# Row maxima and row sums of an attention stage sent through small DMA transfers, and three of four score steps started from a bank that ScalarE has filled

## The reference

```python
def _L0_conv_ref(x, gn_gamma, gn_beta, w_qkv, w_proj, b_proj):
    B, C, H, W = x.shape                      # 2, 256, 64, 64
    nh = NUM_HEADS                            # 4
    d = C // nh                               # 64
    xn = group_norm(x, gn_gamma, gn_beta)
    qkv = jnp.einsum('bchw,oc->bohw', xn, w_qkv).reshape(B, 3, nh, d, H * W)
    q, k, v = (qkv[:, 0], qkv[:, 1], qkv[:, 2])
    scores = jnp.einsum('bhci,bhcj->bhij', q, k) * d ** (-0.5)
    attn = jax.nn.softmax(scores, axis=-1)
    out = jnp.einsum('bhij,bhcj->bhci', attn, v).reshape(B, C, H, W)
    proj = jnp.einsum('bchw,oc->bohw', out, w_proj) + b_proj[None, :, None, None]
    return xn + proj
```

## Time and profile before

| | before |
|---|---|
| median of three runs | 5492.59 us (5486.8 to 5498.76) |
| the profiled execution | 5486.11 us |
| its span in the trace | 5484.3 us |
| TensorE busy | 4957.6 us, 90% |
| VectorE busy | 3959.3 us, 72% |
| GpSimd busy | 2966.1 us, 54% |
| ScalarE busy | 2793.4 us, 51% |
| attention loop, first batch element | 139 to 1333 us of the span |
| attention loop, second batch element | 1498 to 2690 us |

### The profile page before, as it was taken

One profiled execution on the slowest core, in us unless ns is written; L12 is line 12 of the kernel. 1 busy time (PEld: TensorE's weight loads), 2 busy tenths in 40 slices (PEclk: granted clock), 3 DMA queues, 4 the chain that ended last, 5 costly groups with the idle time before them and its releaser, 6 DMA issues. The chain is left out here.

```text
span 5484.3 us, 73719 instructions
## 1 busy us (share of the span) xinstructions
PE 4957.6 (90%) x22320; PEld 2313.6 (42%) x22320; DVE 3959.3 (72%) x6354; ACT 2793.4 (51%) x4750; POOL 2966.1 (54%) x2339
## 2 busy tenths in 40 slices
PE   7999999999899999999978869969978996999788
PEld 3333333333333333333346657745544553554344
DVE  4788888883588888888333334458887886898898
ACT  2666666664266666666411111135544554555455
POOL 0555555555055555555437757746645664665675
PEclk9999999999999999999978879989999998999899
DMA  2000000000000000000134435569969998998998
GB/s 73 1 1 1 1 1 1 1 1 34 30 1 1 1 1 1 1 1 1 37 87 128 128 111 163 162 242 365 388 268 350 371 389 304 378 387 350 396 410 358
DMA packets 320271, 812.24 MB, mean 148 GB/s; under 512 B 70094, under 2 KB 137556, under 8 KB 319758
## 3 DMA queue, kind: packets, MB, share of 16 engines
q0 software_dynamic: 193536, 679.59, 32.8%
q1 hardware_dynamic: 126478, 129.39, 6.9%
HBM read 708.40 MB, written 100.43 MB: 147 GB/s over the span
## 5 line engine op out<-in xcount | busy, mean ns | idle before, releaser
L653 POOL TENSOR_TENSOR arena<-arena 128x1024 f32<-128x1024 f32 x480 | 1168.0, 2433 | 955.2 <-ACT arena L1310 952.6
L1841 DVE TENSOR_REDUCE arena<-ps 128x2 f32<-128x1024 f32 x1024 | 1252.2, 1223 | 457.5 <-PE ps L805 454.2
L705 POOL DMA_INDIRECT arena<-corners,arena x1152 | 1094.2, 950 | 687.6 <-issue 301.6
L1310 ACT ACTIVATE arena<-ps 128x1024 f32<-128x1024 f32 x1024 | 995.4, 1022 | 611.2 <-PE ps L834 609.4
L2065 DVE SCALAR_TENSOR_TENSOR ps<-arena,ps 128x256 f32<-128x256 f32 x2304 | 956.3, 483 | 230.9 <-DVEq L2059 220.9
L1172 PE MATMUL ps<-arena 128*128 128x512 f32 x2304 | 1047.5, 598 | 0.2
L834 PE MATMUL ps<-arena 64*128 64x512 f32 x4096 | 977.9, 590 | 19.0 <-ACT ps L1293 19.0
L847 PE MATMUL ps<-arena 128*64 128x512 f32 x4096 | 991.3, 605 | 0.0
L1503 ACT ACTIVATE ps<-arena 128x256 f32<-128x256 f32 x1152 | 500.2, 469 | 471.0 <-DMA arena<-corners,arena 208.4
L689 POOL DMA_INDIRECT arena<-corners,arena x576 | 544.8, 946 | 275.5 <-issue 244.3
L1860 DVE TENSOR_TENSOR arena<-arena 128x1024 f32<-128x1024 f32 x480 | 630.5, 1314 | 79.3 <-ACT arena L1310 79.3
(11 more groups left out here) (165 smaller groups left out, 4108.5 us busy)
## 6 DMA issues: line engine op xcount, KB each, us to landing
corners<-arena SPq DMA_DIRECT2D x256, 256.0 KB
arena<-corners,arena POOLq DMA_INDIRECT x1728, 7.7
img<-in_x SPq DMA_DIRECT2D x8, 1024.0 KB, 9.3
corners<-arena SPq DMA_DIRECT2D x128, 64.0 KB, 2.2
arena<-in_wd SPq DMA_DIRECT2D x2, 2304.0 KB, 8.5
between<-img SPq DMA_DIRECT2D x4, 1024.0 KB, 5.9
arena<-between SPq DMA_DIRECT2D x4, 1024.0 KB, 10.5
resid<-img SPq DMA_DIRECT2D x8, 512.0 KB, 3.4
```

Source lines behind the costliest of these rows:

```text
L653: pool.tensor_tensor(SUMS[u % 2][:, 0], SUMS[u % 2][:, 0], PAIR[g % 2][:, :, 0], ALU.add).then_inc(sum_a, 2)
L705: pool.indirect_dma_start(G3[4 * k + t].rearrange("p a c -> p (a c)"), None, table256[b], bass.IndirectOffsetOnAxis(ap=IS3[:, k, t:t + 1], ...
L1310: af(P[n % 4].rearrange("p h q -> p (h q)"), ps[:, 2 * (n % 2):2 * (n % 2) + 2, :].rearrange("p h q -> p (h q)"), ACT.Exp, scale=float(D) ...
L1841: v.tensor_reduce(mxp[i % 2][:, :, j], ps[:, 4:6, :], AX.X, ALU.max).then_inc(mx_done, 1)
```

## The change

The maxima no longer pass through TensorE and ScalarE. VectorE joins eight maxima (`MNEG`) and a new small multiply of 128 by 2 elements scales them into f16 (`MROWS`). SyncE sends them, four times for each block, to a row in DRAM (`send_row`), and once for each block reads that row back into all 128 partitions (`spread_rows`) of one of two tables `MWIDE`, laid out as query by head. Both the `COEF` matmuls and the seeds now read `MWIDE`, the first with a step of two elements.

The row sums of all blocks but the last also go through DRAM: `RC` is written out, read back as 128 by 8 elements (`SINV`), inverted by one reciprocal, written out and read back into 128 partitions. GpSimd joins the two partial tables (`fold`), so that `row_sums` is half as long.

ScalarE now seeds three of four steps, and each seed stands right behind the exponential that frees its two banks.

```diff
+        row_buf = nc.dram_tensor("row_buf", (2, 2 * CHUNK), F16, kind="Internal").ap()
+        sum_buf = nc.dram_tensor("sum_buf", (2, CHUNK), F32, kind="Internal").ap()
+        inv_buf = nc.dram_tensor("inv_buf", (2, CHUNK), F32, kind="Internal").ap()
...
-        MWIDE = att.f32(2, CHUNK, dt=F16)
-        MSTAT = att.f32(128)
+        MWIDE = [att.f32(CHUNK, 2, dt=F16) for _ in range(2)]
+        MNEG = att.f32(2)
+        MROWS = [att.f32(4, 2, dt=F16) for _ in range(2)]
+        SINV = att.f32(2, 4)
...
-        def seeds_in(g):
-            return 2 * g + 3 if 2 * g + 3 < STEPS else None
+        def is_seeded(n):
+            return n >= 2 and n % 4 != 0
...
+                def send_row(u, t):
+
+                    sp.wait_ge(mrow_ready, 4 * u + t + 1)
+                    if u >= 2:
+                        sp.wait_ge(wide_ready, 16 * (u - 1))
+                    sp.dma_start(row_buf[u % 2, t * 256:(t + 1) * 256].rearrange("(p h) -> p h", h=2),
+                                 MROWS[u % 2][:, t, :]).then_inc(row_sent, 16)
+
+                def spread_rows(u):
+
+                    sp.wait_ge(row_sent, 64 * (u + 1))
+                    if u >= 2:
+                        sp.wait_ge(p_ready, NT * (u - 1))
+                    sp.dma_start(MWIDE[u % 2].rearrange("p q h -> p (q h)"),
+                                 row_buf[u % 2, :].partition_broadcast(128)).then_inc(wide_ready, 16)
+
+                def send_sums(u):
+
+                    sp.wait_ge(sums_copied, u + 1)
+                    for h in range(2):
+                        sp.dma_start(sum_buf[h:h + 1, :], RC[64 * h:64 * h + 1, :]).then_inc(sums_sent, 16)
+                    sp.wait_ge(sums_sent, 32 * (u + 1))
+                    sp.dma_start(SINV, sum_buf.rearrange("h (p i) -> p h i", p=128)).then_inc(sums_back, 16)
+
+                def spread_inverses(u):
+
+                    sp.wait_ge(rc_done, u + 1)
+                    if u >= 1:
+                        sp.wait_ge(rc_wide, 32 * u)
+                    sp.dma_start(inv_buf.rearrange("h (p i) -> p h i", p=128), SINV).then_inc(inv_sent, 16)
+                    sp.wait_ge(inv_sent, 16 * (u + 1))
+                    for h in range(2):
+                        sp.dma_start(RC[64 * h:64 * h + 64, :],
+                                     inv_buf[h, :].partition_broadcast(64)).then_inc(rc_wide, 16)
+
+                for u in range(BLOCKS + 1):
+                    if u < BLOCKS:
+                        send_row(u, 0)
+                    if u >= 2:
+                        send_sums(u - 2)
+                    if u < BLOCKS:
+                        send_row(u, 1)
+                    if u >= 2:
+                        spread_inverses(u - 2)
+                    if u < BLOCKS:
+                        send_row(u, 2)
+                        send_row(u, 3)
+                        spread_rows(u)
...
+                def fold(u):
+
+                    pool.wait_ge(sum_a, NT * (u + 1))
+                    pool.wait_ge(sum_b, NT * (u + 1))
+                    for h in range(2):
+                        to = SUMS[u % 2][:, h]
+                        pool.tensor_tensor(to[:, 0], to[:, 0], to[:, 1], ALU.add).then_inc(folded, 1)
...
+                    if pair == 0 and u >= 1:
+                        fold(u - 1)
                     if pair == 4 and u + 2 < BLOCKS:
                         cast_queries(u + 2)
                     if pair == 12 and u >= 1:
                         normalized(u - 1)
+                fold(BLOCKS - 1)
                 normalized(BLOCKS - 1)
...
                 def scores(n):
...
                     if kc == 0:
-                        pe.wait_ge(aux_done, aux_at[("rows", 4 * u + 3)] + 1)
+                        pe.wait_ge(wide_ready, 16 * (u + 1))
                     if n >= 2:
                         pe.wait_ge(p_ready, n - 1)
-                    if n % 2 == 0 or n == 1:
+                    if is_seeded(n):
+                        pe.wait_ge(seeded, seeds_before[n] + 1)
+                    else:
                         for h in range(2):
                             rows = slice(64 * h, 64 * h + 64)
-                            mm(ps[:, 2 * (n % 2) + h, :], COEF[rows, :], MROW[u % 2][rows, :], start=True, stop=False,
+                            mm(ps[:, 2 * (n % 2) + h, :], COEF[rows, :], MWIDE[u % 2][rows, :, h], start=True, stop=False,
                                tile_position=(64 * h, 0))
...
                 def seed(n):
 
-                    act.wait_ge(aux_done, aux_at[("wide1", n // NT)] + 1)
+                    act.wait_ge(wide_ready, 16 * (n // NT + 1))
                     act.wait_ge(p_ready, n - 1)
-                    af(ps[:, 2:4, :].rearrange("p h q -> p (h q)"), MWIDE.rearrange("p h q -> p (h q)"), ACT.Copy,
-                       scale=ROW_COEF).then_inc(seeded, 1)
+                    bank = 2 * (n % 2)
+                    af(ps[:, bank:bank + 2, :], MWIDE[n // NT % 2].rearrange("p q h -> p h q"), ACT.Copy, scale=ROW_COEF).then_inc(seeded, 1)
...
                 for g in range(STEPS // 2):
-                    weights(2 * g)
-                    weights(2 * g + 1)
...
-                    if seeds_in(g) is not None:
-                        seed(seeds_in(g))
-                    if rows_in(g) is not None:
-                        row_copy(rows_in(g))
+                    for n in (2 * g, 2 * g + 1):
+                        weights(n)
+                        if n + 2 < STEPS and is_seeded(n + 2):
+                            seed(n + 2)
...
-                    v.tensor_reduce(MSTAT.rearrange("p (h a) -> p h a", h=2)[:, :, 0], mxp[i % 2], AX.X, ALU.max,
-                                    negate=True).then_inc(mstat_ready, 1)
+                    v.tensor_reduce(MNEG, mxp[i % 2], AX.X, ALU.max, negate=True).then_inc(mneg_ready, 1)
+                    dve.wait_ge(mneg_ready, i + 1)
+                    if i % 4 == 0 and i >= 8:
+                        dve.wait_ge(row_sent, 64 * (i // 4 - 1))
+                    v.tensor_scalar(MROWS[i // 4 % 2][:, i % 4, :], MNEG, 1.0 / (HALF_SCALE ** 2 * ROW_COEF), None,
+                                    ALU.mult).then_inc(mrow_ready, 1)
...
-                    if g >= NT // 2 and 3 <= g % (NT // 2) <= 10:
-                        inverse_sums(g // (NT // 2) - 1, g % (NT // 2) - 3)
+                    if g >= NT // 2 and g % (NT // 2) == 6:
+                        inverse_sums(g // (NT // 2) - 1)
```

More of the change, by code:

```diff
@@ L299, in program @@
                 opening.append(("max", i))
[L300 to L305, removed]
         def sums_in(g):
             return g // (NT // 2) - 1 if g >= NT // 2 and g % (NT // 2) == 2 else None
-        def wide_in(g):
-            return g // (NT // 2) + 1 if g % (NT // 2) == NT // 2 - 1 and g // (NT // 2) + 1 < BLOCKS else None
-        def seeds_in(g):
-            return 2 * g + 3 if 2 * g + 3 < STEPS else None
-        aux = [what for what in opening if what[0] == "rows"] + [("wide0", 0), ("wide1", 0)]
-        for g in range(STEPS // 2):
-            if rows_in(g) is not None:
[L319 to L326, removed]
+        def is_seeded(n):
+            return n >= 2 and n % 4 != 0
+        seeds_before = [sum(is_seeded(m) for m in range(n)) for n in range(STEPS + 1)]
         block = ctx.enter_context(nc.Block())
@@ L608, in _ @@
                 inverse_root(grs[:, :])
-                for what, value in ((COEF, 0.0), (MSTAT, 0.0), (ONES, 1.0)):
+                for what, value in ((COEF, 0.0), (ONES, 1.0)):
                     pool.memset(what, value).then_inc(pool_step, 1)
-                pool.wait_ge(pool_step, 3)
-                pool.sem_inc(pool_step, -3)
+                pool.wait_ge(pool_step, 2)
+                pool.sem_inc(pool_step, -2)
                 for h in range(2):
@@ L644, in _ @@
                     if pair == 0 and u >= 2:
-                        pool.wait_ge(aux_ready, aux_at[("sums", u - 2)] + 1)
+                        pool.wait_ge(sums_ready, u - 1)
                     if pair == 0 and u == 1 and b == 0:
@@ L835, in scores @@
                                   QF[u // QB][rows, (u % QB) * CHUNK:(u % QB + 1) * CHUNK], start=False, stop=True,
-                                  tile_position=(64 * h, 0), skip_group_check=n % 2 == 1 and n > 1)
+                                  tile_position=(64 * h, 0), skip_group_check=is_seeded(n))
                     last.then_inc(st_scores, 1)
@@ L851, in row_sums @@
                 def row_sums(u):
[L853 to L868, removed]
+                    pe.wait_ge(folded, 2 * (u + 1))
+                    if u >= 1:
+                        pe.wait_ge(sums_copied, u)
+                    for h in range(2):
+                        last = mm(ps[64 * h:64 * h + 64, 7, :], ONES, SUMS[u % 2][:, h, 0, :], start=True, stop=True,
+                                  tile_position=(0, 64 * h))
+                    last.then_inc(sums_ready, 1)
                 for i in first:
@@ L874, in _ @@
```

(4 more changed lines are left out.)

85 lines of the change are left out of this document (38 added, 47 removed).

## The result

The changed kernel takes 5725.15 us (median of four runs, 5717.73 to 5733.77); the kernel before, beside it on the same chip, took 5489.69. The ratio is 1.0427, with a 95% interval of 1.0406 to 1.0449: 235 us slower, where 80 were forecast. The sign is right, the size is not, and the time lies above the range of 5490 to 5620. The profiled execution took 5717.73 us, its span 5716.0.

What follows compares the result with a forecast made beforehand. The prediction took TensorE, busy 90% of the span, to bound the kernel. Per batch element 120.8 us lost and 81.0 won gave +39.8, +79.6 for both, so 5572 us, range 5490 to 5620.

Steps and rivals of the forecast that it cites:

- The DMAs: Row writes and spread through DRAM for each block: landing in 6.3 us with 7.9 available, so hidden with little to spare.
- rival (c): Rows come late at each block: 11 us for the two transfers, +93, some 5665 us; chance 0.09.
- The price of a late microsecond: At a block's start, every microsecond the rows take beyond the available time costs 30 us in all.
- The order of ScalarE: Attention loop, seeds behind each exponential: scores 3 wait until 5.42 us; four steps take 8.91 against 8.68, 0.23 more.
- GpSimd's collision: Attention loop: VectorE's add waits for GpSimd's later add; four steps 0.76 us over 8.68, 90.4 for 119 groups.
- (b): Attention loop: the adds of VectorE and GpSimd don't collide; -77, 5416 us, faster; chance 0.17.
- The small multiply: VectorE's new multiply in pairs 1, 5, 9, 13 waits for GpSimd: 2.2 us a block, 30.8 for 14 blocks.
- rival (a): VectorE's and GpSimd's adds collide, but VectorE's new multiply doesn't wait for GpSimd: 61.6 less, 5511 us; chance 0.25.
- The steps of two elements: Seeds on ScalarE read MWIDE in steps of two elements; a seed 0.1 us longer would add 24 us.
- (d): Seeds take 0.1 us longer from reading MWIDE in steps of two: +24, 5596 us; chance within the forecast's 0.42.
- What is removed: Transposes, spread tables, row sums and meetings of normalized with add_b that cost TensorE time: 81.0 us won for one batch element.
- The sum: Whole kernel: 120.8 us lost and 81.0 won for an element, +39.8, +79.6 for both, 5572 us; chance 0.42.

Runs made afterwards that it cites:

- probe: Changed kernel with LEAD 42 plus, for each block, a scratch DRAM write of 128 pieces, five sizes or spacings in turn: 5572.0 us in one run.
- fill: Changed kernel (LEAD 36) with five unused f32 matmuls put before each block's wait for the rows: 5692.44 us, ratio 1.0363 to the kernel before.
- noadd_nomul: Changed kernel with LEAD 42, without the multiply of two elements and without GpSimd's adds (output not the reference's): 5461.34 us, ratio 0.9944.
- best: Changed kernel with LEAD 42, both exponentials of a pair before its seeds, and no multiply of two elements: 5409.64 us, ratio 0.9842.
- lead42: Changed kernel with the leading pass six steps further ahead (LEAD 42 in place of 36): 5561.18 us, ratio 1.0127 to the kernel before.
- pack16: Changed kernel (LEAD 36) with one write of 16-byte pieces for each block, MWIDE read in steps of 16 bytes: 6374.82 us, ratio 1.1602.

## Why the prediction was wrong

**The failed step is "The DMAs".** It put 3.5 for a row and 2.8 for the spread, 6.3 us, against 7.9 available: "Hidden, with little to spare". They take 7.6 and 4.8, 12.4 us, and TensorE waits 4.4 at each block. The time available was right (7.93 measured), so it is the landing times that failed, both of them: 4.1 too short for the row, 2.0 for the spread. The mechanism stood as rival (c), with 0.09, and the sentence that spoke for it, that pieces of 4 bytes are smaller than anything in the earlier trace rows, was the one to weigh. As `probe` shows, these writes are a kind by themselves, and the earlier trace rows bound them from one side only. With an upper end of 12 the range would have reached 5572 + 4.1 x 30 = 5695, still short of the result by the clock's share.

**The price of a late microsecond**, 30 us, holds for the wait: 31 waits of 4.4 us in the mean sum to 135.6. Not in the working was that TensorE comes out of the wait at the lower clock: 33 more, by `fill`.

**The order of ScalarE** was right: 5.42 to scores 3 where 5.42 was worked out, a group of 9.37 against 9.44. Without the collision 9.02 was measured against 8.91. The 0.11 lies behind scores 3: in the trace of `noadd_nomul` the next leading step starts 0.93 after them and the values 0.35 after that, where 0.855 and 0.31 were taken.

**GpSimd's collision** was right in place and sign, and (b) is out: 186 of 480 `add_b` last 1.4 us or more in the changed kernel, some 90 of them about 2.25, against 60 in the kernel before. Its share is 0.35 of the 0.69 in a group, not 0.53 of 0.76.

**The small multiply** does wait (rival (a) is out), 1.20 us in the mean over 39 between 400 and 1200 us. The reduce before it, 0.17 at 694.61, is not held by the same add. What the multiply costs in the changed kernel itself, where the term was 2.2 for each block, no run tells; at `LEAD` 42 it was 1.1 with the changed order and 2.3 with late seeds.

**The steps of two elements** cost nothing: seeds take 1.03, so (d) is out.

**What is removed** was not tried by itself. `best`, where the two adds no longer meet, is 83 us under before, 41.5 for an element. Of the 81.0 its `normalized` keeps 10.9 (0.77 idle for each block, as in the earlier trace rows) and its halved row sums 15 x 0.95 = 14.3, which leaves 55.8. The traces show where the other 14 are. From the first to the last scores of an element `best` takes 1122.4 us against 1178.7, 56.3 less, near the term, though groups of 8.61 in place of 8.68 are in it too. The rest is lost outside the loops. The opening is 8.7 longer for each element (93.9 against 85.2), the price of `LEAD` 42; in this one pair of traces the stretch between the loops is 4.5 longer and the layers behind them, which no edit touches, 14.7, and why stays open.

**The sum** without late rows: +79.6 forecast, +70 measured in `lead42`, inside the stated range. That is partly luck. In its trace the two loops are only 48 us longer than before the change (1203 against 1179 for each), since the collision costs less than its term and the multiply, in other pairs, half of its own, and the openings, not in the sum, add 17.

## What to carry to other kernels

When work moves from an engine to a DMA, the landing time of that very form of transfer (piece size, spacing) decides; where the trace has no such row, one scratch transfer of the form measures it. The waits of TensorE measured here were paid twice, once as time and once at the lower clock behind them, so it pays to give late data more lead before anything else is tuned. A tiny instruction of VectorE between SBUF and SBUF can inherit the whole of a GpSimd instruction, and dropping it was worth 34 us in one order and 72 in another.

## What the hardware showed beside that

- 128 packed pieces of 4 bytes into DRAM land in 6.9 to 7.6 us (medians); the same pieces 512 bytes apart in 1.4, packed pieces of 16 to 512 bytes in 1.4 to 1.5.
- One row of 2 KB read from DRAM into 128 partitions, 256 KB in all, takes 4.8 us (3.8 in `pack16`), and the plain load of 288 KB 2.8.
- A source of f16 read in steps of 16 bytes doubles a ScalarE copy (1.03 to 2.02 us) and makes two matmuls 1.06 instead of 0.39; steps of 4 bytes are free.
- After 4.3 us without work TensorE's granted clock is 0.64 over the next 6.2 us.
